# Who issues the output stores of a two-phase batched-matmul kernel: SyncE among its loads, or ScalarE behind its own copies

## The reference

```python
def _L0_cond_ref(x, weight, bias, lora_a_weights, lora_b_weights, scaling_factors, adapter_id):
    base = jnp.einsum('bsi,oi->bso', x, weight) + bias
    a_sel, b_sel = lora_a_weights[adapter_id], lora_b_weights[adapter_id]
    scale = scaling_factors[adapter_id]
    low = jnp.einsum('bsi,bri->bsr', x, a_sel)
    delta = jnp.einsum('bsr,bor->bso', low, b_sel)
    return base + scale[:, None, None] * delta

def _L1_cond_ref(x, weight, adapter_ids):
    w = weight[adapter_ids]
    return jnp.einsum('bij,bkj->bik', x, w)

x = x + _L0_cond_ref(x, ..., itok_B_1_7)     # 8 adapters
x = x + _L1_cond_ref(x, ..., itok_B_1_14)    # 16 weights; the batches use 14 of them
```

## Time and profile before

| | |
|---|---|
| median of three runs | 2582.23 us (2581.29 to 2582.72) |
| profiled execution, first to last instruction | 2580.0 us |
| TensorE busy | 2558.7 us, 99% |
| VectorE busy | 2122.4 us, 82% |
| ScalarE busy | 1386.0 us, 54% |
| GpSimd busy | 766.4 us, 30% |
| granted TensorE clock | 0.999 |

### The profile page before, as it was taken

The page is one execution under the profiler, slowest core; times in us unless marked ns, Lnnn a source line. Parts: engine busy times, 40 slices in busy tenths (PEclk is TensorE's granted clock), DMA queues, the critical chain, the costliest instruction groups (busy, mean ns, idle before and its releaser), DMA issues.

```text
span 2580.0 us, 35474 instructions
## 1 busy us (share of the span) xinstructions
PE 2558.7 (99%) x12250; PEld 2116.2 (82%) x12250; DVE 2122.4 (82%) x1926; ACT 1386.0 (54%) x1478; POOL 766.4 (30%) x614
## 2 busy tenths in 40 slices
PE   8999999999999999999999999999999999999999
PEld 7888888888888888878888888888888888888887
DVE  6568999997888999898787887787877877887865
ACT  3324333334443333467676676766766666766755
POOL 5554332432433425220330231311311312213311
PEclk9999999999999999999999999999999999999999
DMA  9996642963576538878678677787899999998986
GB/s 357 350 379 197 201 138 96 291 212 131 169 244 210 161 131 252 300 262 276 245 257 297 240 264 276 251 275 257 295 356 351 353 348 359 352 322 320 315 321 228
DMA packets 213714, 686.19 MB, mean 266 GB/s; under 512 B 23424, under 2 KB 31776, under 8 KB 213536
## 3 DMA queue, kind: packets, MB, share of 16 engines
q1 hardware_dynamic: 204032, 649.33, 70.1%
q0 software_dynamic: 9216, 33.56, 6.8%
q10 hardware_dynamic: 288, 1.05, 0.1%
HBM read 650.29 MB, written 100.66 MB: 291 GB/s over the span
## 4 chain that ended last, share of the span: by engine, by line
PE 93%; DVE 4%; DMA 2%; issue 1%; ACT 0%; SPq 0%; POOL 0%; DVEq 0%; ACTq 0%; POOLq 0%
PE acc L1291 18%; PE acc L1292 17%; PE acc L1293 17%; PE acc L1208 13%; PE acc L1209 13%; PE acc L1210 13%; DMA xst<-xt 1%; DVE ws L1162 1%; PE acc L1225 1%; PE acc L1247 1%; DVE tx L1162 1%; DMA bias_s<-bias 1%; DVE acc L1151 0%; DMA wb<-w 0%; DVE acc L1088 0%
## 5 line engine op out<-in xcount | busy, mean ns | idle before, releaser
L1162 DVE TENSOR_TENSOR ws<-wb,ws 128x1024 fp32r<-128x1024 f32 x968 | 1262.1, 1331 | 282.7 <-ACT ws L998 266.8
L998 ACT CAST ws<-wb 128x1024 fp32r<-128x1024 f32 x968 | 990.8, 1050 | 783.2 <-PE acc L1293 473.2
L1291 PE MATMUL acc<-ws,ops 128*128 128x512 f32 (+1 forms) x2048 | 800.3, 391 | 2.4 <-DVE ops L1162 2.1
L1292 PE MATMUL acc<-ws,ops 128*128 128x512 f32 (+1 forms) x2048 | 798.3, 390 | 0.0
L1293 PE MATMUL acc<-ws,ops 128*128 128x512 f32 (+1 forms) x2048 | 797.7, 390 | 0.0
L908 POOL TENSOR_TENSOR wb<-wb,eye_s 128x128 f32<-128x128 f32 x384 | 332.6, 897 | 1153.0 <-DMA wb<-w 1152.9
L1208 PE MATMUL acc<-tx,ws 128*128 128x512 f32 x1600 | 623.4, 390 | 3.6 <-DVE tx L1162 1.7
L1210 PE MATMUL acc<-tx,ws 128*128 128x512 f32 x1600 | 622.5, 389 | 0.0
L1209 PE MATMUL acc<-tx,ws 128*128 128x512 f32 x1600 | 622.5, 389 | 0.0
L1291 PEld LDWEIGHTS acc<-ws,ops 128*128 128x128 f32 x2048 | 384.9, 188 | 81.8 <-issue 4.6
L1293 PEld LDWEIGHTS acc<-ws,ops 128*128 128x128 f32 x2048 | 384.8, 188 | 80.5
(11 more groups left out here) (67 smaller groups left out, 1019.5 us busy)
## 6 DMA issues: line engine op xcount, KB each, us to landing
wb<-w SPq DMA_DIRECT2D x816, 512.0 KB, 6.3
xb<-x SPq DMA_DIRECT2D x78, 512.0 KB, 5.6
xb<-x POOLq DMA_DIRECT2D x64, 512.0 KB, 8.8
y<-acc SPq DMA_DIRECT2D x32, 1024.0 KB, 10.1
wb<-w_sums SPq DMA_DIRECT2D x64, 512.0 KB, 7.8
out<-ost SPq DMA_DIRECT2D x128, 256.0 KB, 7.3
xst<-xt SPq DMA_DIRECT2D x60, 512.0 KB, 6.1
ystage<-y SPq DMA_DIRECT2D x60, 512.0 KB, 7.1
```

The costliest lines, as they stand in the source:

```text
L998: eng.copy(hi, src).then_inc(s_hi, 1)
L1162: eng.tensor_tensor(lo, src, hi, ALU.subtract).then_inc(s_lo, 1)
L1291: eng.matmul(dst, yh, wh, start=begin, stop=False)
L1292: eng.matmul(dst, yh, wl, start=False, stop=False)
```

## The change

The 128 stores leave SyncE's list and are issued by ScalarE, each right behind its copy: ScalarE waits until its own copy is complete (`s_ev1`), then issues the store. For the destination it needs the batch numbers of the group, so it loads four registers once per group, at the group's first copy. The wait for all stores at the end of the program moves to ScalarE as well. Copies, sizes, staging tiles and all other tasks and their due times stay.

```diff
-        for kc in range(C1):
-            for b in range(G):
-                end = te[at["S", q, kc, NU - 1, max(0, b - 1)]]
-                loads.append((end + 3.0, "out", (q, kc, b)))
...
-                elif kind == "out":
-                    q, kc, b = index
-                    i = out_no(q, kc, b)
-                    batch = order(0, q)[b]
-                    eng.wait_ge(s_ev1, i + 1)
-                    dst = out[bass.ds(batch, 1), :, PART[kc] * 512:PART[kc] * 512 + 512]
-                    eng.dma_start(dst.rearrange("a p n -> (a p) n"), ost[:, i % NOST, :]).then_inc(s_out[i % NOST], 16)
...
-            for k in range(NOST):
-                eng.wait_ge(s_out[k], 16 * (NB * C1 // NOST))
-
...
+            batch_of = {}
             for key, what, n, index in scalar_tasks:
                 if what == "ev1":
...
                     eng.copy(ost[:, n % NOST, :], s_bank(kc, b)[:]).then_inc(s_ev1, 1)
+                    if q not in batch_of:
+                        if q == 0:
+                            eng.wait_ge(s_order, 4)
+                        batch_of.pop(q - 1, None)
+                        batch_of[q] = load_order(eng, 0, q)
+                    eng.wait_ge(s_ev1, n + 1)
+                    dst = out[bass.ds(batch_of[q][b], 1), :, PART[kc] * 512:PART[kc] * 512 + 512]
+                    eng.dma_start(dst.rearrange("a p n -> (a p) n"), ost[:, n % NOST, :]).then_inc(s_out[n % NOST], 16)
                     continue
...
                 src, hi, _ = split_views(kind, index)
                 eng.copy(hi, src).then_inc(s_hi, 1)
+            for k in range(NOST):
+                eng.wait_ge(s_out[k], 16 * (NB * C1 // NOST))
```

## The result

The changed kernel takes 2587.34 us (median of 9 runs, 2585.74 to 2589.92) against 2581.29 us before (9 runs, 2580.56 to 2583.56, the three known to the forecast among them). The ratio is 1.0024 with a 95% interval of 1.0014 to 1.0033: the change costs 6.05 us by the medians, clear of noise and small. The forecast was 8.0 us.

A forecast was written before the change was run, and what follows sets the result against it. TensorE, busy 2558.7 of 2580.0 us, bounds the kernel, so only making it wait matters. Seven stalls (6.8) plus the end (1.2) make 8.0 us, 2588.0 of span, forecast 2590.2; its own range 2585.5 to 2596, 8 in 10 2581.5 to 2599.

The forecast's parts named there:

- the border of 2587.4: Time above which a measurement counts as slower: 0.2%, 5.2 us, from no change; slower had 0.57, same 0.37, faster 0.06.
- The place: Column block 1 to 2, groups 0 to 6: TensorE stalls 0.97 us at each of seven places, 6.8 us in all.
- The price of a cycle: ScalarE, copy start to next task: copy 0.58, hand-off 0.2, issue 0.44, next task 0.08; 1.30 us, range 1.15 to 1.6.
- The margin: Column block 1 to 2: VectorE's tile is ready 1.87 us before TensorE begins with it; stall = 4 x cycle - 2.36 - 1.87.
- What was costed at nothing: Column blocks 2 to 3, 0 to 1 and group to group: delays covered by margins, 0 us.
- the 0.6 us set aside for the load: Column block 0 to 1, once per group: register load adds perhaps 0.6 us, 1.6 at the read's maximum; covered.
- The end: Last group: fourth copy and last store 1.2 us late, with no later work to hide it.
- The rival that the two issuers contend: ScalarE's issues held up by SyncE's weight-load issues: another 0.3 us per cycle, 2601 us; chance 0.13.
- The gain from a relieved SyncE: SyncE loses 128 issues: taken as 0; rival faster (2577) had the `xst` waits vanish, -4.0 us, chance 0.06.

## Why the prediction was nearly right

- **The forecast as a whole**: 2587.34 lies within its range of 2585.5 to 2596, near the lower end, and just under the border of 2587.4 that the prediction had drawn between slower (0.57) and same (0.37). The mechanism is settled by the runs; to be called slower by that border or not was a matter of luck.
- **The place**, right: one wait of TensorE on the S block of step 2 in column block 2, in groups 0 to 6, and nowhere else in a column block. Putting those 28 stores back removed it, moving those 28 alone brought it.
- **The price of a cycle**, the mis-sized term: taken as 1.30 us, measured 1.19 (1763.87 - 1762.68). The copy (0.58) and the hand-off to the issue (0.17) were right; the issue was 0.34 and not 0.44. I had taken ScalarE's two DMAs at the program's start because it was the same engine; SyncE's 128 stores with their median of 0.357 were the nearer row, since they are the same transfer (at the program's start SyncE's own first two DMAs take 0.40 and 0.41 us as well); with 0.357 the cycle would have been 1.22 and the stall 0.64. By the formula 1.19 gives 4 x 1.19 - 4.23 = 0.53 us per stall; the column blocks grew by 0.7. The rest is the slow restart of TensorE (0.34 for 0.24 us) and the last 0.05 us of the margin, which remain between the tile's end and the matmul. Two errors per stall, 0.4 us too much by the cycle and 0.2 too little by these two, left 5.1 where 6.8 was forecast; that they partly cancel is luck.
- **The margin**, right: 1.87 us, and it is gone.
- **What was costed at nothing**: right. In column block 0 to 1, where the register load stands (0.31 us for the read in the median), no wait appears: at group 3 the read begins at 1716.48, beside the cast that precedes the copy, and the copy's cycle is 1.20 us, so the 0.6 us set aside for the load were not spent; the low-rank block keeps 1.0 us of its 2.79, since the copy of bank 7 comes 1.8 us later; column blocks 1 and 3 have the old times to 0.01 us.
- **The end**: forecast 1.2, measured 0.8, again three cycles of 1.19 instead of 1.30.

ScalarE's last copies, beside the earlier trace rows; the last one starts 3.53 us after the first, before 2.72:

```profile
2577.29 0.59 ACT L910 COPY ost<-acc 128x512 f32<-128x512 f32 x1 [6.16 <-PE acc L1290]
...
2580.82 0.58 ACT L910 COPY ost<-acc 128x512 f32<-128x512 f32 x1 [0.59 <-ACT ost L910]
2581.57 0.34 ACTq L918 DMA_DIRECT2D out<-ost  x1
```

- **The rival that the two issuers contend**, not borne out: the duration of ScalarE's issue shows no trace of SyncE's.

```profile
L918 ACTq DMA_DIRECT2D out<-ost x128: 338/339/372, 1169.8 to 2581.6; - x128
```

It is 0.339 us in the median and 0.372 at most. Of the 128 issues 44 run while SyncE issues a DMA too; they also take 0.339 us in the median and 0.372 at most. One of the 128 (at 1720.79) begins 0.3 us later than usual. Longer issues (up to 1.10 us behind all four copies, up to 1.18 in two halves) were seen only where ScalarE issued several in a row, some of them with no issue of SyncE beside them (0.86 us and less). The lock wait of which the Trainium skill tells (Perfetto Trace Analysis, section "DMA Instruction — HWDGE (DVE, Sync)") shows in the duration of none of the 128.
- **The gain from a relieved SyncE**, rightly taken as 0: with 124 stores off its list and no stall the ratio is 1.0003 (0.9994 to 1.0012). The Trainium skill's rule that another issuer saves issue time alone (DMA: Bandwidth & Descriptors, section "Issuing engines are not separate DMA queues") agrees with that. Nothing here excludes a gain of 1.5 us or less.
- **A step of the reasoning that was too simple**: I added the wait and the issue as if each cost its time on ScalarE. The wait alone cost 0.13 us; wait and issue together, taken when casts were in hand, cost 0; right behind each copy they cost 0.71 (1.19 - 0.48). The wait empties the engine, which sits idle for 0.60 us behind each copy (the brackets of the timeline), and the issue has nothing beside which it could run. The sum was right for this kernel, where every next task stands behind both, and would have been wrong elsewhere.

What stays open: what sets the `xst` waits, 0.5 to 4.0 us, from one execution to the next, why one group in seven (group 2, and group 6 when only the tight place was ScalarE's) took 0.3 us more than the others, and why group 0 kept its clock with two issues per store.

## What to carry to other kernels

Where a helper engine feeds a saturated one, its busy share says little: look for the place where a tile's last preparation lies closest to its first use, and add up what the edit puts in front of that preparation. A store right behind the copy that it depends on is dear on the copying engine (0.71 us a copy here), because the wait for completion drains the engine before the issue; put some other work between the copy and its store, and the same engine issued it at no cost that could be measured. No gain from relieving SyncE could be measured here; no wait of TensorE had ended at a store.

## What the runs showed of the hardware

- A store issue on ScalarE runs beside ScalarE's own compute: 0.86 us for two issues while casts followed each other at 0.96 us without a gap. Its sequencer runs ahead of the engine: three issues began before a copy that stands ahead of them in the list.
- Issues of ScalarE and SyncE at the same time did not lengthen ScalarE's: 0.339 us in the median with (44) and without (84).
- TensorE's clock: behind a pair of waits (1.36 to 1.98 us, then 0.75) with one pair of matmuls between them, the granted clock was 0.50 (1.2 GHz) for 3.4 us in six places of seven, and cost 1.7 us each time, two thirds of the stall itself; in the seventh, behind 1.40 and 0.75 us, it stayed at 1.00. Behind a single wait of 2.1 us at the change of phases it fell in some executions (before, at 1117) and not in others (changed kernel, at 1118). Behind the shorter single waits of these two traces it stayed at 1.00: up to 1.7 us for `xst` in the kernel before, 0.40 to 0.70 for weight tiles in the changed kernel, here in the 3.4 us behind one of them:

```profile
1776.10:1779.50 3.40, 3.37 (x15) 2.80 (x16) 3.40 (x4) 3.40 (x5) 0.00 (x0) 1.00 0.96 347
```

So two issues per store in place of one were six times as dear (37 us for 6).
